# Node rows of a graph network worked out pair by pair inside the third propagation layer

## The reference, cut to what matters

```python
for _ in range(3):                                   # L0
    x0 = segment_sum(x0[src], dst) / max(counts, 1)
x = layernorm(x_in + x0)
def mlp(x, Wh, bh, Wo, bo, w, b):                    # three hidden layers of 64
    for i in range(3): x = relu(x @ Wh[i] + bh[i])
    x = x @ Wo + bo
    return layernorm(x) * w + b
fs, fr = mlp(x[src], flux...), mlp(x[dst], flux...)  # 128 wide: two numbers a feature
a = mlp((x[src] + x[dst]) / 2, a...)                 # 64 wide
flux = (fs . nvec + fr . nvec) / 2 - a * (x[src] - x[dst]) / 2
out = layernorm(x + x + segment_sum(flux, dst))
```

## Time and profile before

| | |
|---|---|
| median of three runs | 7836.83 us |
| the profiled execution, its own time | 7838.55 us |
| its span in the trace | 7836.7 us |
| PE / DVE / ACT / POOL busy, share of the span | 75% / 43% / 36% / 69% |
| layer two, first to last dense matmul | 1715.9 to 2451.8 us |
| layer three | 2454.8 to 3213.6 us |
| node stage, to the first work of the edge stage | 3213.6 to 3471.0 us |
| edge stage and final norm | 3471.0 us to the end |

### The profile page before, as it was taken

How to read it: one execution, slowest core, us unless ns; L and a number is a source line. 1 busy time by engine, 2 the same in 40 slices (tenths; PEclk the granted TensorE clock), 3 DMA queues, 4 the chain that set the end, 5 groups by cost and what they waited for, 6 DMA issues and landing times. The chain is left out here.

```text
span 7836.7 us, 213920 instructions
## 1 busy us (share of the span) xinstructions
PE 5910.6 (75%) x80407; PEld 4886.7 (62%) x80407; DVE 3335.9 (43%) x6012; ACT 2816.6 (36%) x5153; POOL 5380.7 (69%) x5216
## 2 busy tenths in 40 slices
PE   0159999999999999757777777777777777777770
PEld 0159999989999999524555555555555555555550
DVE  5469989952221111463333333333333333333337
ACT  0168888850000000113444333343333434433440
POOL 5776766647776777217777777777777777777760
PEclk9999999999999999768888888888888888888885
DMA  5234434346665566325555555555555555555545
GB/s 118 73 114 146 145 129 145 130 176 226 215 228 212 206 216 219 114 86 132 137 138 136 136 136 137 137 137 136 136 136 137 138 136 137 137 136 136 137 120 153
DMA packets 647894, 1155.36 MB, mean 147 GB/s; under 512 B 396199, under 2 KB 454503, under 8 KB 629524
## 3 DMA queue, kind: packets, MB, share of 16 engines
q0 software_dynamic: 217440, 521.49, 26.8%
q1 hardware_dynamic: 419168, 593.46, 23.1%
q10 hardware_dynamic: 10212, 25.35, 1.0%
HBM read 931.86 MB, written 207.96 MB: 145 GB/s over the span
## 5 line engine op out<-in xcount | busy, mean ns | idle before, releaser
L1635 POOL DMA_INDIRECT edge_rows<-node_table,edge_et x3224 | 3137.7, 973 | 983.0 <-issue 944.6
L798 POOL DMA_INDIRECT two_rows<-x_parts,src_at x1120 | 1085.3, 969 | 477.8 <-issue 371.9
L1079 PE MATMUL two_acc<-x_parts,two_win 128*128 128x192 bf16 x16072 | 1355.8, 247 | 32.2 <-DMA two_win<-adjacency 16.8
L1079 PEld LDWEIGHTS two_acc<-x_parts,two_win 128*128 128x128 fp8e4 x16072 | 1340.8, 99 | 35.8 <-issue 33.6
L1822 DVE TENSOR_TENSOR edge_zx<-edge_zp,edge_rows 128x512 f32<-128x512 f32 x403 | 278.9, 692 | 2142.3 <-ACT edge_z L1734 2086.5
L1663 PE MATMUL edge_mp<-edge_h,edge_W 128*128 128x512 f32 x1612 | 1124.7, 837 | 0.0
L978 ACT ACTIVATE one_win<-one_count 128x784 fp8e4<-128x784 f32 x1312 | 1073.8, 824 | 135.2 <-PE one_count L939 63.9
L798 POOL DMA_INDIRECT one_rows<-x_parts,src_at x560 | 834.8, 1491 | 335.1 <-PE one_edge_acc L1002 170.4
L1721 ACT ACTIVATE edge_yc<-edge_rows 128x512 f32<-128x512 f32 x403 | 254.0, 630 | 2213.0 <-DMA edge_rows<-node_table,edge_et 2213.0
L1695 PE MATMUL edge_seg<-edge_seg,edge_edge_now 128*1 128x66 f32 x6448 | 292.4, 228 | 839.9 <-ACT edge_seg L1750 839.2
L925 PE MATMUL one_acc<-x_parts,one_win 128*128 128x192 bf16 x8036 | 858.5, 246 | 0.5 <-ACT one_win L978 0.5
(11 more groups left out here) (289 smaller groups left out, 10477.3 us busy)
## 6 DMA issues: line engine op xcount, KB each, us to landing
two_win<-adjacency SPq DMA_DIRECT2D x82, 3136.0 KB
adjacency<-one_win SPq DMA_DIRECT2D x41, 3136.0 KB
edge_near<-near_ids SPq DMA_DIRECT2D x403, 192.0 KB
edge_rows<-node_table,edge_et POOLq DMA_INDIRECT x3224
node_sums<-edge_seg SPq DMA_DIRECT2D x806, 33.0 KB
two_rows<-x_parts,src_at POOLq DMA_INDIRECT x1120
end_sums<-node_sums SPq DMA_DIRECT2D x7, 1848.0 KB
edge_yd<-y_parts SPq DMA_DIRECT2D x806, 12.0 KB
```

Source lines behind the costliest of these rows:

```text
L798: pool.indirect_dma_start(rows[:, b % 2, i * GB + d, :], None, XP.rearrange("p (j c) -> (p j) c", c=3 * C), bass.IndirectOffsetOnAxis(ap=s ...
L1079: mm = pe.matmul(acc[b][:, half * 3 * C:(half + 1) * 3 * C], win[:, b, half, j, :].bitcast(FP8), now[:, j, :], start=(j == 0), stop=(j == ...
L1635: pool.indirect_dma_start(rows[:, h.b, t, :], None, T5, bass.IndirectOffsetOnAxis(ap=et[:, h.b, 0, t:t + 1].bitcast(I32), axis=0))\
```

## The change

`node_rows` is gone. `later_layers` treats the third layer's 49 pairs as items, each one after the other: an edge item every five steps, and a dense item every step. DVE takes a pair's sums, adds x and norms them right when they are done; PE works through the pair's f32 products in five stages, at fixed places among the 196 dense matmuls of the next step (an item alone: from matmul 120 on, 18 apart; with an edge item, that one from matmul 20 on); ACT and DVE do the rest, two rings of six rows (`row`, `y3`) hold the results, and SP stores a pair's rows four steps later, between window loads. The weights and x are loaded at the start of layer two on ACT's DMA queue, and the weights are prepared by DVE after two steps of layer two. The node-table copy of the normed x moves from POOL to ACT. The two halves of the edge sums share one PSUM bank now, and the ids of a block (`near_at`) and the order of gathering are laid out so that first one half's 35 columns and then the other's come; the counts of matmuls, gathers and selections are the same.

```diff
-                later_layers(nc, A, XP2, XP3, x_parts, x3, rcnt, src_at, near_at, values)
-                nc.all_engine_barrier()
-                node_rows(nc, x, x3, T5, Y3, eps_col, ident, fWh, fbh, fWo, fbo, flw, flb, aWh)
+                later_layers(nc, A, XP2, XP3, x_parts, rcnt, src_at, near_at, values, x, T5, Y3, eps_col, ident,
+                             fWh, fbh, fWo, fbo, flw, flb, aWh)
...
+def items(h):
+
+    edge = [Item(h, 1)] if h.place % PARTS == 0 and not early(h, 1) else []
+    return edge + [Item(h, 0)]
...
         @block.scalar
...
+            act.dma_start(x_own[:, 0:J - 1, :], x[0:(J - 1) * P, :].rearrange("(j p) c -> p j c", p=P)).then_inc(loaded, 16)
...
+            def node(it):
+                act.wait_ge(sems["squares"], it.n + 1)
+                act.activation(stat[:, :], stat[:, :], ACT.Sqrt, bias=eps_col[:, 0:1], scale=1.0 / C).then_inc(sems["rooted"], 1)
+                if from_item(it, 1):
+                    flux_root(it.n - 1)
+                    act.wait_ge(sems["y_ready"], it.n)
+                act.wait_ge(sems["turned"], it.n + 1)
+                act.activation(xT[:, :], tp, ACT.Copy).then_inc(sems["x_ready"], 1)
+                if from_item(it, RN):
+                    act.wait_ge(row_stored[it.slot], 32 * it.turn)
+                act.activation(row[:, it.slot, :, 0:C], xn[:, it.slot, :, :], ACT.Copy).then_inc(sems["x_copied"], 1)
+                for i in range(3):
+                    act.wait_ge(sems["m_ready"], 3 * it.n + i + 1)
+                    act.activation(hT[i][:, :], hp[i], ACT.Relu, bias=bh[:, i:i + 1]).then_inc(sems["h_ready"], 1)
+                act.wait_ge(sems["o_ready"], it.n + 1)
+                act.activation(flux_sq[:, :, :], flux_ps[it.b2], ACT.Square).then_inc(sems["sq_ready"], 1)
...
         @block.sync
...
+            def step(h):
+                load(h, 1)
+                if not early(h, 4):
+                    for it in items(h.back(4)):
+                        store(it)
...
         @block.tensor
...
+            stages = (turn, first, lambda it: hidden(it, 1), lambda it: hidden(it, 2), last)
...
+                due = items(h.back(1)) if layer and not early(h, 1) else []
+                for at in range(2 * J):
+                    half, j = at // J, at % J
+                    if at == J and not early(h, 1):
+                        edge_sums(pe, h.back(1), sel, rows, edge_acc, sel_ready, fetched, edge_made, used, layer)
+                    for it, begin in zip(due[::-1], (120, 20)):
+                        if at >= begin and (at - begin) % 18 == 0 and (at - begin) // 18 < len(stages):
+                            stages[(at - begin) // 18](it)
+                            pe.sem_inc(issued, 1)
+                    mm = pe.matmul(acc[b][:, half * 3 * C:(half + 1) * 3 * C], win[:, b, half, j, :].bitcast(FP8),
+                                   now[:, j, :], start=(j == 0), stop=(j == J - 1))
+                mm.then_inc(summed, 1)
...
+            for it in items(Chunk(0, DP - 1, 2 * PARTS)):
+                for run in stages:
+                    run(it)
...
         @block.vector
...
+            def norm(it, sums, done):
+
+                oi.at(base + it.n * LINKS - (LINKS - FIRST_LINKS) if from_item(it, 1) else base)
+                own = xn[:, it.slot, :, :]
+                if from_item(it, RN):
+                    dve.wait_ge(sems["x_copied"], it.n - RN + 1)
+                oi.link(dve.tensor_reduce(xw[:, :, :], sums, AX, ALU.add))
+                dve.sem_inc(done, 1)
+                oi.link(dve.tensor_tensor(own, xw[:, :, :], scale_of(it.at), ALU.mult))
+                oi.link(dve.tensor_tensor(own, own, x_own[:, bass.ds(it.at, 2), :], ALU.add))
+
+                def root():
+                    dve.sem_inc(sems["squares"], 1)
+                    if from_item(it, 1):
+                        variance(it.n - 1)
+                    dve.wait_ge(sems["rooted"], it.n + 1)
+                layer_norm(oi, dve, own, square[:, :, :], stat[:, :], mean_col[:, :], eps_col, root, C)
+                dve.sem_inc(sems["normed"], 1)
...
+            def nodes(h):
+                todo = items(h)
+                for i, it in enumerate(todo):
+                    edge = i + 1 < len(todo)
+                    if edge:
+                        dve.wait_ge(used, BLKS + h.c)
+                        norm(it, edge_pairs, edge_made)
+                    else:
+                        dve.wait_ge(summed, DP + h.c + 1)
+                        norm(it, pairs_of(acc[1 - h.b2]), made)
+                        if not isinstance(h.c, int) or h.c < BLKS:
+                            pick(dve, h, sel, values, near_at, used, sel_ready, BLKS)
+                    if from_item(it, 1):
+                        m, slot, turn, b2 = before(it)
+                        flux(m, slot, turn, b2, from_item(it, RN + 1))
```

More of the change, by code:

```diff
@@ L93 @@
 BLKS = HQ * PARTS
+RN = 6
 X_Y, X_F0, X_F1 = C, 2 * C, 2 * C + W6
@@ L999, in edge_sums @@
         pe.wait_ge(edge_made, layer * HQ + b.fifth)
-    for i in range(2):
-        for d in range(GB):
-            mm = pe.matmul(edge_acc[:, i, 0:3 * C], sel[:, b.b2, d, :, i], rows[:, b.b2, i * GB + d, :],
-                           start=(m == 0 and d == 0), stop=(m == PARTS - 1 and d == GB - 1))
+    for e in range(2 * GB):
+        i, at = (m * 2 * GB + e) // GC, (m * 2 * GB + e) % GC
+        mm = pe.matmul(edge_acc[:, i * 3 * C:(i + 1) * 3 * C], sel[:, b.b2, e // 2, :, e % 2], rows[:, b.b2, e, :],
+                       start=(at == 0), stop=(at == GC - 1))
     mm.then_inc(used, 1)
@@ L1025, in later_layers @@
         sel = sb("sel", [P, 2, GB, P, 2], BF16)
[L1026 to L1030 removed]
+        x_own = sb("x_own", [P, J, C])
@@ new lines, in later_layers @@
+        xn, row = sb("xn", [P, RN, 2, C]), sb("row", [P, RN, 2, W5])
+        y3 = sb("y3", [P, RN, 2, 3, C], BF16)
+        xT, hT = sb("xT", [P, P]), [sb(f"h{i}", [P, P]) for i in range(3)]
+        square, flux_sq = sb("square", [P, 2, C]), sb("flux_sq", [P, 2, 2 * C])
+        mean_col, stat, ssq = sb("mean", [P, 2]), sb("stat", [P, 2]), sb("ssq", [P, 2])
+        W, WY, WO = sb("W", [P, 3, P]), sb("WY", [P, P]), sb("WO", [P, 2, 2 * C])
+        wo, bo, wmean = sb("wo", [P, 2 * C]), sb("bo", [P, 2 * C]), sb("wmean", [P, 1])
@@ L1051, in _, with load @@
+            def nodes(h):
+                for it in items(h):
+                    node(it)
+            chunks(act, nodes, DP, 2 * PARTS)
+            flux_root(PAIRS - 1)
         @block.sync
         def _(sp):
-            for layer in range(2):
-                def step(h):
-                    if layer or not early(h, 2):
-                        sp.wait_ge(summed, layer * DP + h.c - 1)
-                    sp.dma_start(win[:, (h.b + layer) % 2, :, :, :].rearrange("p h j n -> p (h j n)"),
-                                 A[bass.ds(h.c * P, P), :]).then_inc(brought[(h.b + layer) % 2], 16)
-                chunks(sp, step, DP, 2)
+            def load(h, layer):
+                b = (h.b2 + layer) % 2
+                if layer or not early(h, 2):
+                    sp.wait_ge(summed, layer * DP + h.c - 1)
+                sp.dma_start(win[:, b, :, :, :].rearrange("p h j n -> p (h j n)"), A[bass.ds(h.c * P, P), :]).then_inc(brought[b], 16)
@@ new lines, in _ @@
+            chunks(sp, lambda h: load(h, 0), DP, 2)
+            def step(h):
[3 more added lines that the diff above has]
+                        store(it)
+            chunks(sp, step, DP, 2 * PARTS)
+            for c in range(DP - 4, DP):
+                for it in items(Chunk(0, c, 2 * PARTS)):
+                    store(it)
+            for b in range(RN):
+                sp.wait_ge(row_stored[b], 32 * len(range(b, PAIRS, RN)))
@@ new lines, in last @@
+            def last(it):
+                pe.wait_ge(sems["h_ready"], 3 * it.n + 3)
+                if from_item(it, 2):
+                    pe.wait_ge(sems["o_used"], it.n - 1)
+                to = flux_ps[it.b2].rearrange("p j c -> p (j c)")
+                pe.matmul(to, ones[0:1, :], bo2[0:1, :, :].rearrange("p j c -> p (j c)"), start=True, stop=False)
+                pe.matmul(to, hT[2][:, :], WO[:, :, :].rearrange("p h c -> p (h c)"), start=False, stop=True).then_inc(sems["o_ready"], 1)
@@ new lines, in step @@
+            def step(h):
+                if not early(h, 1):
+                    pick(dve, h.back(1), sel, values, near_at, used, sel_ready, 0)
+                    if h.place % PARTS == 0:
+                        k = h.fifth - 1
+                        oe.at(k * 8)
+                        dve.wait_ge(used, h.c)
+                        mean(oe, edge_pairs, 2 * k, edge_made)
+                o.at(h.c * 8)
+                dve.wait_ge(summed, h.c + 1)
+                mean(o, pairs_of(acc[h.b2]), 2 * h.c + 2 * HQ, made)
@@ new lines, in _ @@
+            for c in range(2):
+                step(Chunk(0, c, 2 * PARTS))
+            oi = Chain(dve, item_order)
```

(24 more changed lines are left out.)

396 lines of the change are left out of this document (136 added, 260 removed).

## The result

The changed kernel takes 7707.1 us (median of 4 runs, 7704.94 to 7720.89) against 7835.2 us for the kernel before (4 runs, 7819.5 to 7843.65): a ratio of 0.9843, with 0.9823 to 0.9862 as its 95% interval. Forecast were 7698 us, range 7662 to 7775. The profiled execution after is the longest of the four: own time 7720.89, span 7719.2.

The account below looks back on a forecast made before the run. Layer three was taken as bound by PE and gathers neck and neck, the node stage by no engine. Base 723.5, items 108, edge waits 21 and end 20 replace 1016.2 us; plus 3 gives -140.7: 7698 us, range 7662 to 7775.

Parts of the forecast that it names:

- The sign and the size: Whole kernel: faster, chance 0.93, by 140.7 us against the profiled execution, to 7698 us.
- The base: Layer three without the added items: 758.8 us falls to 723.5, as 35 us of gather waits and slower clock go.
- An item at 2.3 us: PE in layer three: f32 products 2.04 us plus 0.05 per group; 47 items in the stream cost 108 us.
- The edge pair: Layer three, seven steps behind an edge pair: PE waits 2.2 us for DVE's selection, slow matmuls add 0.8; 21 us.
- The loop's issue gap, 2.3: Layer three on PE: 2.3 us of issue wait, counted in the base as staying.
- The start of layer two: Loading x shares the DMA engines with the second window: 3 us more, between 0 and 15.
- The end: From the last dense matmul to the edge stage, two remaining items take 20 us (17 to 30).
- Groups that wait: Rival: PE's groups in layer three each cost some 0.5 us, not 0.05; 106 us more, 7795; chance 0.11.
- Gathers held by DVE, by its small instructions or all of it: Two rivals, layer three: small DVE instructions hold gathers, 7778, chance 0.07; gathers as slow as layer one's, 7896, chance 0.05.
- Hidden work (7663): Rival: gathers bound layer three, so PE's items cost less, 2.0 us each without edge waits; 7663 us, chance 0.05.

Follow-up runs that it names:

- half the gathers: Kernel before, with only 7 of the 14 gathers of each block issued in layer three: 7798.37 us, ratio 0.9953.
- the three edits together: Changed kernel with selection ahead of the norm, weights prepared after eight layer-two steps, not two, and flux bias as bf16 product: 7630.22 us, ratio 0.9738.

## Why the prediction was right, and where it missed

**The sign and the size: right.** The mechanism is the one forecast. A stage that used no engine well (257.4 us) went into a layer in which DVE and ACT had room, and came back as PE time at 2.3 us an item.

**The base: the mechanism right, the size partly by luck.** Forecast were 35 us of gather waits and slow matmuls behind them that a longer PE step hides. They are hidden: the changed kernel has 6.7 us of such waits left, the first two, as forecast. But 35 was what was left over, and not all of it gathers. In the trace of before, the steps with a gather wait, and those behind, exceed 17.32 us by 29 in all after the first two waits; another 6.5 us lie in the two steps in which the loop turns, where I had 2.3. The first of these has no gather wait in it and lasts 21.43:

```profile
2844.32 1.32 PE L1002 MATMUL two_edge_acc<-two_rows,two_sel 128*128 128x192 bf16 x14
...
2865.75 1.32 PE L1002 MATMUL two_edge_acc<-two_rows,two_sel 128*128 128x192 bf16 x14
```

That half the gathers gave 34.7 doesn't settle it either, since that kernel also loses most of the first two waits (0.9 us of 7.6 is left), which my base kept.

**An item at 2.3 us: right by its sum, not by its parts.** I had 2.04 of products and 0.05 for each of five groups. The runs show no cost at the first four groups, and one bias product of 0.63 where I had 0.44, a flux product of 0.53, and 0.09 ahead of them. Exchanging the bias for a bf16 product took off 0.71. Whether the bias is dear for its single row of weights, for its f32 passes or for being the first f32 product behind dense matmuls is not separated.

**The edge pair: right place, mis-sized.** "2.2 us x 7 = 15, and 0.8 x 7 = 6: 21" measured 4.5 x 7 = 32. The chain from the flux product's end (2707.95) to PE's start (2711.23) is 3.3 us, where I had 2.65. Of the 0.6 more, 0.24 go by behind the selection, and 0.36 in DVE's pause ahead of it. The slow step I took from a single row behind a wait of 2.4 us, as 17.15 - 16.33 for the dense matmuls alone, and left out the edge block itself, whose next row starts 2.01 us on instead of 1.15. Both together are 1.7 in the earlier trace rows too. The granted clock shows it here; two windows of the changed kernel, with the wait of 2.35 us at the edge block that starts at 2606 in the first (the one of the seven that is put down to issue):

```profile
2600.00:2620.00 20.00, 17.65 (x169) 15.88 (x168) 7.82 (x25) 3.20 (x10) 11.32 (x12) 0.91 0.36 116
2620.00:2640.00 20.00, 20.00 (x230) 19.32 (x228) 8.11 (x26) 2.55 (x8) 11.16 (x11) 1.00 0.60 208
```

**The loop's branch: missed.** "The loop's issue gap, 2.3" is what a wait list gave. In the changed kernel it is 6.7 us in four pieces, with steps of 28.65 where others of their kind have 24.9. In the kernel with half the gathers it is 4.2 us each time. Before, it was there too, 4.1 us in one step and 2.4 in the other (there the list puts PE's stop down to DVE), and I had counted most of it as gather waits that go. It stayed. That the branch is the cause is read from the place, not tested.

Edge pairs +11, items +2 and the branch +4.4 are 17.4 of the 18.1 us in layer three.

**The start of layer two: too small, and the wrong mechanism.** I charged 3 us for transfers that meet. The second and third step are 11.8 us longer than before, beyond the 10 that I had named as a sign of being wrong, and the layer as a whole 7.4. It was a queue. ACT issues the load of x, and DVE, whose program has the weight preparation between its second and third step, waits for that load with the selection behind it. PE then waits for the selection.

```profile
1731.52 26.31 ACTq L1096 DMA_DIRECT2D two_x_own<-in_x  x1
...
1769.72 0.29 DVE L1267 TENSOR_REDUCE two_wmean<-two_wo 128x1 f32<-128x128 f32 x1 [8.96 <-DMA two_x_own<-in_x]
...
1772.59 1.09 DVE L987 TENSOR_TENSOR two_sel<-values,near_at 128x1792 bf16<-128x1792 bf16 x1
1773.82 2.40 PE L1000 MATMUL two_edge_acc<-two_rows,two_sel 128*128 128x192 bf16 x14 [8.54 <-DVE two_sel L987]
```

The issue takes 26 us on ACT, where I had 15 from SP. "DVE's 4 us of weight preparation fall between two steps, where it idles" failed as a step: DVE idles in sum, but what matters is whether its next instruction for PE stands behind something late. Six steps later the load has landed, and the three edits together have layer two 16.6 us shorter; 11 to 12 of these are the steps at this place. Most of the rest are gather waits, 2.8 us instead of 8.7, and these differ from one execution to the next (9.3 before, 5.6 in the trace of the result).

**The end: 26.8 instead of 20.** The chain of the last two items runs in the order forecast, each hop longer. The dense item's norm is done at 9.9 us behind the last dense matmul (8.4 forecast), its PE chain at 17.0 (12.6), its flux part at 22.4 (16), and the edge stage begins 4.4 us behind that (3.5). So 3 of the 7 us lie in the PE chain. The bias product takes 1.22 us at the lower clock (0.59 over this stretch), where 0.69 stands in the layer, and behind ACT it waits 0.46 more:

```profile
3338.05 0.49 PE L1214 MATMUL two_acc<-x_parts,two_win 128*128 128x192 bf16 x4
...
3348.54 0.48 PE L1173 MATMUL two_turned<-ident,two_xn 128*128 128x128 f32 x1 [2.73 <-DVEq L1337]
3353.21 1.22 PE L1191 MATMUL two_flux<-two_bo,two_ones 1*128 1x256 f32 x2 [0.46 <-ACT two_h L1125]
...
3365.29 0.30 SPq L1601 DMA_DIRECT2D edge_base_i<-bases  x1
```

I had priced a lone chain with durations from a stretch in which PE never stops.

**The rivals.** Groups that wait: none does at 18 matmuls, and at 2 they cost 1.70 us an item, so it is the spacing that keeps this rival away. Gathers held by DVE, by its small instructions or all of it: with DVE's busy time four times that of before, the gathers of layer three last 981 ns, not 968, which is 7 us over 560 and shows in no wait of PE. The rule of the Trainium skill ("SBUF — State Buffer", section "SBUF: two separate sides"), that certain DVE instructions and a GpSimd operation lock each other out of a shared port pair for a whole instruction, would have given some 4 us a block if taken to the letter for all casts and two-input products. For instructions of 0.2 to 0.3 us this trace doesn't bear it out. Only beside the 1.09 us selection is a gather seen stretched: in layers two and three of either kernel, none that starts outside a selection takes over 1.3 us. Hidden work (7663): the gather waits did go, but PE's items are paid in full.

## What to carry to other kernels

Before moving a small stage into a full one, price it on the engine that has no room, and look for the cover of each hop: here 1.5 us of dense work covers a chain of 0.6. Then read the order of instructions on each helping engine for the one instruction that the busy engine waits for, and put it ahead of all that waits itself, norm and one-time preparation alike; that and one cheaper bias product were worth another 80 us. An engine's idle share says nothing about what stands behind what.

## What the runs showed of the hardware that was not expected

- The same kernels took 7.6 to 7.8 ms on one chip and 11.7 to 11.9 ms on three others. In the longer executions PE idles for 500 to 750 us in layers two and three without a releaser in the profile, and a change that gives 1.6% on the one gives nothing there. One execution of 12050.2 us came on the chip of the 7.8 ms executions, but with a granted clock of 1.00 over the whole, where the others have 0.75 to 0.76; whether it is the same thing is open.
- Where a loop of ten steps turned, the step was 4.2 us longer on PE, each time, in a stretch of 83 ns matmuls.
- A stop of 2.8 us cost a further 1.7 us, in slower matmuls behind it. Around a like stop of 2.35 us the granted clock was 0.91 over 20 us.
- An f32 product of one row of weights and 256 columns, first of its group, held PE for 0.63 us by the starts, a bf16 one of 128 rows in its place for 0.11.
